# Recurrence of a test-time-training layer: the row term's centring on GpSimd, output rows transposed in place

## What is computed

```python
def step(carry, inp):
    W1c, b1c = carry
    xq, xk, xv, et = inp
    Z1 = xk @ W1c + b1c
    grad = _ln_l2_bwd(Z1, xv - xk, g, bb)
    Attn1 = jnp.tril(xq @ xk.swapaxes(-1, -2))
    b1_bar = b1c - jnp.tril(et) @ grad
    Z1_bar = xq @ W1c - et * Attn1 @ grad + b1_bar
    last_eta = et[..., -1, :, None]
    W1n = W1c - (last_eta * xk).swapaxes(-1, -2) @ grad
    b1n = b1c - (last_eta * grad).sum(-2, keepdims=True)
    return ((W1n, b1n), xq + _ln(Z1_bar, g, bb, EPS_IN))
```

## Time and profile before

| | us |
|---|---|
| three runs | 571.07, 572.27, 575.37 |
| median | 572.27 |
| the profiled execution | 577.86 |
| its span in the profile | 576.0 |
| busy in it: PE, DVE, ACT, POOL | 489.2, 428.6, 347.4, 327.4 |

### The profile page before, as it was taken

The page is one execution under the profiler, slowest core; times in us unless marked ns, Lnnn a source line. Parts: engine busy times, 40 slices in busy tenths (PEclk is TensorE's granted clock), DMA queues, the critical chain, the costliest instruction groups (busy, mean ns, idle before and its releaser), DMA issues.

```text
span 576.0 us, 30352 instructions
## 1 busy us (share of the span) xinstructions
PE 489.2 (85%) x12556; PEld 319.1 (55%) x12556; DVE 428.6 (74%) x1526; ACT 347.4 (60%) x1166; POOL 327.4 (57%) x590
## 2 busy tenths in 40 slices
PE   0699899998578988898888888888896699998996
PEld 0344344444466776777777666667675344455663
DVE  4756888898566588898888888888865667676552
ACT  3344444323366588888888899988765487553321
POOL 1276999989244366666665655566753677330112
PEclk9999999999677599999999999999978899998998
DMA  8300111112011111111111000101100500000223
GB/s 338 126 24 15 37 38 36 38 41 56 15 28 26 25 30 28 38 28 33 32 28 27 2 1 1 37 19 38 37 19 4 172 1 2 1 2 1 74 75 146
DMA packets 15136, 24.74 MB, mean 43 GB/s; under 512 B 4228, under 2 KB 4968, under 8 KB 15080
## 3 DMA queue, kind: packets, MB, share of 16 engines
q1 hardware_dynamic: 15080, 24.10, 13.7%
HBM read 11.50 MB, written 4.19 MB: 27 GB/s over the span
## 4 chain that ended last, share of the span: by engine, by line
PE 30%; DVE 25%; ACT 10%; issue 8%; POOL 1%; POOLq 0%; ACTq 0%
PE PS L1168 6%; PE PS L925 4%; PE PS L1256 3%; PE PS L907 3%; PE PS L361 3%; ACT work L1557 3%; DVE work L1342 2%; DVE work L1337 2%; DVE work L1323 2%; DVE work L1301 2%; PE PS L1153 2%; PE PS L1195 2%; DVE work L1320 2%; DVE PS L1339 2%; PE PS L1180 2%
## 5 line engine op out<-in xcount | busy, mean ns | idle before, releaser
L1168 PE MATMUL PS<-work 32*32 32x32 f32 x4064 | 61.1, 197 | 37.0 <-DVE work L1342 23.4
L1168 PEld LDWEIGHTS PS<-work 32*32 32x32 f32 x4064 | 55.6, 111 | 42.7 <-issue 42.2
L1412 POOL TENSOR_TENSOR work<-work,mask 128x256 f32<-128x256 f32 x64 | 46.7, 730 | 44.2 <-ACT work L1532 44.2
L1301 DVE TENSOR_REDUCE work<-work 128x4 f32<-128x128 f32 x64 | 18.3, 286 | 57.8 <-ACT work L1557 57.8
L512 PE MATMUL PS<-X,work 128*128 128x512 f32 x128 | 60.5, 618 | 0.3 <-ACT X L435 0.3
L1424 POOL TENSOR_TENSOR work<-work,lrh 128x4 f32<-128x4 f32 x64 | 12.9, 202 | 75.7 <-DVE work L1315 70.2
L1153 PEld LDWEIGHTS PS<-work 64*32 64x32 f32 x2048 | 35.0, 115 | 26.7 <-issue 25.5
L1153 PE MATMUL PS<-work 64*32 64x64 f32 x2048 | 46.2, 233 | 3.2 <-issue 2.3
L664 POOL TENSOR_TENSOR work<-work 128x512 f32<-128x512 f32 x32 | 43.9, 1372 | 8.1 <-DVE work L582 8.1
L1195 PE MATMUL PS<-cst 128*128 128x256 f32 x126 | 47.7, 462 | 0.0
L1180 PE MATMUL PS<-work 32*64 32x32 f32 x2016 | 44.7, 227 | 0.3 <-issue 0.3
(11 more groups left out here) (162 smaller groups left out, 1331.7 us busy)
## 6 DMA issues: line engine op xcount, KB each, us to landing
X<-in_x SPq DMA_DIRECT2D x4, 1024.0 KB, 8.0
TK<-KP SPq DMA_DIRECT2D x64, 64.0 KB, 1.9
X<-QP SPq DMA_DIRECT2D x64, 64.0 KB, 2.0
TK<-in_x SPq DMA_DIRECT2D x16, 256.0 KB, 2.8
out<-TK SPq DMA_DIRECT2D x16, 256.0 KB, 2.4
work<-in_rope SPq DMA_DIRECT2D x2, 512.0 KB, 9.2
cst<-in_consts SPq DMA_DIRECT2D x1, 289.0 KB, 4.9
work<-in_wk SPq DMA_DIRECT2D x1, 256.0 KB, 11.2
```

The costliest lines, as they stand in the source:

```text
L1168: mm = nc.tensor.matmul(PS[HD * a:HD * a + HD, bank, b * width:b * width + HD], AM[p][HD * a:HD * a + HD, b, part, :, :].rearrange("p e t ...
L1412: nc.gpsimd.tensor_tensor(AM[p].rearrange("p b s e t -> p (b s) e t"), S1[p].unsqueeze(2).broadcast_to([P, 2 * B, E, CS]), mask2.rearrange ...
```

## The change

In each chunk the addition `YC = YL + cc0` is issued by GpSimd, behind its row product YL, instead of by VectorE. GpSimd can't take it from where `cc0` lay, in PSUM, so `cc0` is moved to SBUF. VectorE's transpose reads ZN and writes its result straight into the rows of TT, in runs of 16 elements; the tile ZT, its semaphore, and ScalarE's `out_store` go, and with them VectorE's waits for the stores behind the last chunk. GpSimd's `out_norm` waits for the transpose as before, by the other semaphore.

```diff
-        cc0, sums = PS[:, 7, at:at + B], PS[:, 7, at + B:at + 3 * B]
+        cc0, cc1 = carve(B), carve(B)
+        sums = PS[:, 7, at:at + 2 * B]
...
                 def out_turn(c):
                     dve.wait_ge(q["zn"], c + 1)
-                    nc.vector.transpose(ZT.rearrange("p b d -> p (b d)"), ZN.rearrange("p b d -> p (b d)")
-                                        ).then_inc(q["zt"], 1)
+                    nc.vector.transpose(
+                        TT.rearrange("p e (b n) -> p b e n", b=B)[:, :, :, c * CS:(c + 1) * CS],
+                        ZN.rearrange("p b (e t) -> p b e t", e=E)).then_inc(q["ot"], 1)
...
-                    dve.wait_ge(q["yl"], c + 1)
-                    dve.wait_ge(q["cy"], c + 1)
-                    nc.vector.tensor_tensor(YC, YL, bc(cc0), ALU.add).then_inc(q["yc"], 1)
                     dve.wait_ge(q["c"], c + 1)
                     nc.vector.tensor_tensor(WX, ZC, bc(cc1), ALU.mult).then_inc(q["w"], 1)
...
                     nc.gpsimd.tensor_tensor(YL, YY[:, 0, :, :], bc(lead[:, 0, :]), ALU.mult).then_inc(q["yl"], 1)
+                    pool.wait_ge(q["yl"], c + 1)
+                    pool.wait_ge(q["cy"], c + 1)
+                    nc.gpsimd.tensor_tensor(YC, YL, bc(cc0), ALU.add).then_inc(q["yc"], 1)
...
                     nc.scalar.activation(SQ, zb, ACT.Square).then_inc(q["sq"], 1)
-                    if past(c, 5):
-                        out_store(c - 5)
                     if past(c, 2):
                         out_square(c - 2, p)
```

More of the change, by code:

```diff
@@ L761, in build @@
         ZQ = [carve(B, HD) for _ in range(3)]
-        SQQ, ZN, ZT = (carve(B, HD) for _ in range(3))
+        SQQ, ZN = (carve(B, HD) for _ in range(2))
         ss, sz, ssq, sd1 = (carve(B) for _ in range(4))
@@ L766, in build @@
         lead = carve(2, B)
-        cc1 = carve(B)
+        cc0, cc1 = carve(B), carve(B)
         def bc(v, n=HD):
@@ L1099, in build @@
             names = ("init my cy updw wcopy bcopy kt2 qt2 qr kr khx base qbase corr s1 am p sq ss sz zc v sd r ts y yp m u u2 "
-                     "yl c w yc gl upd attn zq sqq ssq sdq rq zn zt ot").split()
+                     "yl c w yc gl upd attn zq sqq ssq sdq rq zn ot").split()
             q = {n: sem(f"scan_{n}") for n in names}
@@ L1355, in _ @@
                 out_var(NC - 2)
-                dve.wait_ge(q["ot"], NC - 4)
                 out_turn(NC - 4)
@@ L1362, in _ @@
                 out_r(NC - 1)
-                dve.wait_ge(q["ot"], NC - 3)
                 out_turn(NC - 3)
@@ L1366, in _ @@
                 dve_scale(dve, 0)
-                dve.wait_ge(q["ot"], NC - 2)
                 out_turn(NC - 2)
-                dve.wait_ge(q["ot"], NC - 1)
                 out_turn(NC - 1)
@@ L1418, in out_norm @@
                     if past(c, 1):
-                        pool.wait_ge(q["zt"], c + 0)
+                        pool.wait_ge(q["ot"], c + 0)
                     nc.gpsimd.tensor_tensor(ZN, ZQ[c % 3], bc(sdq[1 - p]), ALU.mult).then_inc(q["zn"], 1)
@@ L1545, in out_sd @@
                     nc.scalar.activation(sdq[1 - p], ssq, ACT.Sqrt, bias=eps6, scale=1.0 / HD).then_inc(q["sdq"], 1)
[L1547 to L1551, removed]
                 def body(c, p):
@@ L1616, in _ @@
                 out_square(NC - 2, 0)
-                out_store(NC - 5)
                 out_sd(NC - 2, 0)
-                out_store(NC - 4)
                 out_square(NC - 1, 1)
@@ L1623, in _ @@
                 out_sd(NC - 1, 1)
-                out_store(NC - 3)
                 act_square(act, 1, False)
                 act_affine(act, 0)
-                out_store(NC - 2)
-                out_store(NC - 1)
                 act.wait_ge(q["ot"], NC)
```

## The result

Over 20 executions of each the changed kernel has a median of 576.44 us and the kernel before 572.67; the ratio is 1.0058, with a 95% interval of 1.0037 to 1.0080. So it is slower by about 3.3 us, where 3.7 less was forecast, and the time lies just outside the stated range. The profiled execution took 575.57 us, its span is 573.8. That is less than the span of before, 576.0, though the kernel is slower: two profiled executions can't be compared by their totals here, since they differ by where and for how long TensorE's clock was at half. In 140 to 220 us alone the granted clock lies between 0.77 and 0.89 in the traces of this case, at 0.77 in before and 0.83 in the changed kernel.

The account below looks back on a forecast made before the run. The recurrence's ring of TensorE, ScalarE and VectorE was taken to bound the kernel. -4.3 us from centring and +0.6 at chunk 56 sum to -3.7, taking 572.27 to 568.6 us, with a range of 564.0 to 575.8.

Parts of the forecast that it names:

- What bounds an ordinary chunk: Recurrence: a ring of TensorE's correction, ScalarE's square and VectorE up to the gradient, with VectorE's centring L1337 on the chain.
- The jump back of TensorE's loop as its own time: In 10 chunks the 0.76 us gap before the correction is TensorE's own, so an earlier gradient gives nothing.
- full gain: Rival: jump-back gap follows the gradient and GpSimd is in time; 45 x 0.16 = 7.2 less, 565.1 us; chance 0.13.
- The addition's length: GpSimd's new addition in each chunk takes 0.40 us, like its twin, the product L1429.
- GpSimd too slow: Rival: the gradient waits for GpSimd's addition, over 0.53 us long; at 0.62, 3.6 us more, 575.9; chance 0.13.
- The estimate of 0.58: GpSimd's addition at twice VectorE's 0.29 us: the gradient comes 0.05 late and the kernel 2.3 us slower.
- the handovers: Around GpSimd's addition: 0.08 us from the coefficient to GpSimd, 0.03 from GpSimd's sum to VectorE's gradient.
- 33 x 0.13 = 4.3: Gradient starts at 263.41 instead of 263.54, gaining 0.13 us in each of 33 chunks: 4.3 us less.
- 0.6 us more: GpSimd's queue at chunk 56, with two long residual additions, grows by 0.58 us and delays TensorE's base matmuls.
- a rival with 0.08: Clock rival: one more stretch of TensorE at half clock costs 6.5 us, giving 575.1; chance 0.08.
- The collision at L1309: Rival: GpSimd's query copy runs into VectorE's L1309, holding it 0.13 us in 33 chunks; 573.2 us; chance 0.06.
- The cover for stores and transposes: Dropped ScalarE stores become idle time and VectorE's idle 0.35 us before L1301 covers longer transposes: 0 us.

Follow-up runs that it names:

- late_first: Changed kernel with wait order swapped on GpSimd (coefficient first) and at the gradient (GpSimd's sum first); 573.45 us, ratio 1.0016 to the kernel before.
- center_only: Kernel before with only the centring moved to GpSimd; transposes and stores as before; 575.29 us, ratio 1.0034 to the kernel before.
- grad_late_first: Changed kernel with the waits swapped at the gradient alone, GpSimd's sum first; 572.72 us, one run.
- add_late_first: Changed kernel with the waits swapped on GpSimd's addition alone, VectorE's coefficient first; 574.83 us, one run.
- not56: Changed kernel with the centring of chunk 56 alone back on VectorE; 573.85 us, ratio 1.0003 to the kernel before.
- only56: Changed kernel with the centring back on VectorE except in chunk 56, coefficient in SBUF for all chunks; 584.56 us, ratio 1.0203 to the kernel before.
- only56_psum: Changed kernel with centring on GpSimd in chunk 56 alone, coefficient in PSUM in the other 63; 575.34 us, ratio 1.0043 to the kernel before.
- late_first_not56_psum: Changed kernel with both wait pairs swapped, chunk 56 centred on VectorE with its coefficient in PSUM; 570.13 us, ratio 0.9979 to the kernel before.
- turn_only: Changed kernel with the addition back on VectorE and its coefficient back in PSUM; 573.10 us, ratio 0.9997 to the kernel before.
- before_again: Kernel before, unchanged, run once more for a second trace; 574.92 us, one run.
- late_first_not56: Changed kernel with both wait pairs swapped and chunk 56 centred on VectorE; 569.77 us, ratio 0.9957 to the kernel before.

## Why the prediction was wrong, step by step

- What bounds an ordinary chunk: right. L1337 was on the chain, and where the gradient came 0.08 us earlier, 2.76 instead of 2.84 behind the start of the sum of squares (late_first), the chunk was 0.09 shorter.
- The jump back of TensorE's loop as its own time: right. Those chunks take 4.46 to 4.54 us in before, in the changed kernel and in those whose other chunks are 3.98. The rival "full gain" falls, by these chunks and by the total. The eight chunks bound by ScalarE stay at 4.58 to 4.60 too.
- The addition's length: right, 0.40, so the rival "GpSimd too slow" falls in the form that I gave it. The estimate of 0.58 from the Trainium skill's page (GPSIMD Engine Reference, Engine selection) does not fit this trace either: 0.40 against VectorE's 0.29.
- **The step that failed first: the handovers.** I took 0.08 to GpSimd from L1412, and 0.03 to VectorE from L1329. Both wait first for the semaphore that comes last. The two new waits have it second. They measured 0.15 and 0.10, so the term "33 x 0.13 = 4.3" is 0. With both mended (late_first) the gain was 0.09 a chunk, and the stretch from chunk 8 to 55 took 201.3 us instead of 203.8, 2.5 less for the 30 ordinary chunks in it.
- **The step that failed second: "0.6 us more" at chunk 57.** The length of the delay was right (1.75 - 1.12 = 0.63), its consequence was not: chunks 56 and 57 take 10.87 us instead of 9.77, 1.1 more, and the clock falls. In the five traces with GpSimd's addition in chunk 56 (changed, center_only, late_first, grad_late_first, add_late_first) the granted clock in 404 to 416 us is 0.57 to 0.77. In the seven without it, it is 0.86 to 1.00; two of these have a fall near there, before from 415 us on and not56 for 3.4 us from 412.5 on. Over the longer stretch of 400 to 470 us the clock is 0.78 to 0.88 in those five and only56, and 0.88 to 0.93 in the seven. I had this as a rival with 0.08 and gave the stall ahead of the fall as its reason, but priced it as chance.
- How the 3.3 us divide: in the 69 timed executions of the kernel before that came with the experiments the time falls by 2.9 us for each 0.01 of mean granted clock. The changed kernel's 20 have 0.950 where those have 0.957 to 0.960 (the clocks of the 20 executions of before that ran with it are not on record), which is 2.0 to 2.9 us. The rest, 0.4 to 1.3, is of the size of what chunk 57 itself loses. This division is a regression and not an experiment. That the loss as a whole comes from chunk 56 is what not56 and only56_psum show; that its clock part does is argued. Against it: late_first_not56_psum, without the long stall, had a mean clock of 0.953 where its batch of before had 0.960, and gained 1.2 us instead of the 2.5 or more that its chunks give. Why its clock was lower is open.
- The collision at L1309: right for ordinary chunks (L1310 takes 0.28 there), and 0.48 instead of 0.42 in chunk 57. The time that I gave for this rival, 573.2, is 572.9 by its own terms (572.27 + 0.6). The cover for stores and transposes: right, 0 within the 0.3% of turn_only's interval.

## What to carry to other kernels

Before an instruction is moved to an engine with time to spare, look for the one place where that engine's queue is already late: one addition of 0.4 us there, in one chunk of 64, made the whole kernel 0.43% slower, several times its own length. By the traces a good part of that is the lower clock behind TensorE's stall; how much is not shown. A handover's price is read from a row whose awaited semaphore stands at the same place among the waits. And compare kernels whose clock falls differently by chunk lengths and medians, not by two profiled spans.

## What the runs showed of the hardware

- The order of two waits before one instruction mattered where one came late. Standing first it was answered in 0.08 us on GpSimd (late_first, add_late_first) and 0.03 on VectorE (grad_late_first), standing second in 0.15 and 0.10 (the changed kernel).
- A VectorE addition of 128 x 128 with both operands in SBUF took 0.50 to 0.52 us next to a GpSimd instruction of 0.61, and 1.18 next to a pair of 2.54; with one operand in PSUM, at the same place, 0.29. The Trainium skill (SBUF — State Buffer, Who interferes with whom) says that a VectorE instruction with two SBUF inputs contends with a GpSimd one that reads SBUF, and one with at most one SBUF input does not. The traces agree: 0.50 against 0.29. I had used the rule for L1309 only, and did not see that the coefficient's place in PSUM had kept the old centring clear of it.
- In the same five traces and in only56 TensorE was idle 1.74 to 1.81 us ahead of its base matmuls of chunk 57, and the granted clock fell to half (1.2 GHz) between 0.3 us ahead of the end of that stall and 2.6 behind it, for 6.8 to 20.5 us. In four with a stall of 1.04 to 1.12 us (before, before_again, turn_only, late_first_not56_psum) it fell nearby in one, before, 2.7 us behind the stall's end and for 10.2 us. In not56 and late_first_not56 the idle time lies ahead of the correction, 1.24 and 1.32 us, and the clock fell in not56 alone, 1.9 us behind it and for 3.4 us. No run varied the stall alone in steps, so where it begins to matter is open.
